# x_t in the order of the product's blocks, and wh in more banks, in a two-layer graph attention kernel

## What is computed

```python
def _gat_layer(x, W, adj):
    proj = x @ W                       # W: 256 x 512
    Wh, Ws = jnp.split(proj, 2, axis=-1)
    scores = Wh @ Ws.T                 # 4096 x 4096
    a = jax.nn.softmax(scores, axis=-1) * adj
    out = a @ Wh
    out = out + x
    return jax.nn.leaky_relu(out, 0.01)

y = _gat_layer(_gat_layer(x, W[0], adj), W[1], adj)
return _layernorm(x + y, axis=-1)      # eps 1e-5
```

## Time and profile before

| | us |
|---|---|
| median of 3 runs | 1680.99 (1677.59 to 1681.62) |
| the profiled execution's own time | 1675.62 |
| its span in the profile | 1673.7 |
| TensorE busy in the span | 1588.3 |
| VectorE | 1233.2 |
| GpSimd | 917.6 |
| ScalarE | 678.8 |
| mean granted TensorE clock | 0.99 of full speed |

### The profile page before, as it was taken

How to read it: one execution, slowest core, us unless ns; L and a number is a source line. 1 busy time by engine, 2 the same in 40 slices (tenths; PEclk the granted TensorE clock), 3 DMA queues, 4 the chain that set the end, 5 groups by cost and what they waited for, 6 DMA issues and landing times.

```text
span 1673.7 us, 23474 instructions
## 1 busy us (share of the span) xinstructions
PE 1588.3 (95%) x8104; PEld 1319.3 (79%) x8104; DVE 1233.2 (74%) x1558; ACT 678.8 (41%) x1175; POOL 917.6 (55%) x935
## 2 busy tenths in 40 slices
PE   7899999999999999999788999999999999999996
PEld 6778888888788888887677888888788888877885
DVE  4567777777777777777636788778878888787785
ACT  4333444444434444444333444344434444434442
POOL 2355555555555555555444555555555555555565
PEclk9999999999999999999999999999999999999998
DMA  5357767777767776768913777777677777777774
GB/s 182 86 147 185 193 185 184 186 198 182 184 186 192 184 186 187 195 186 220 261 32 105 193 192 184 192 201 194 177 191 202 196 186 189 197 190 185 199 192 126
DMA packets 167750, 302.59 MB, mean 181 GB/s; under 512 B 39760, under 2 KB 68432, under 8 KB 167504
## 3 DMA queue, kind: packets, MB, share of 16 engines
q1 hardware_dynamic: 105808, 132.75, 32.3%
q0 software_dynamic: 36864, 134.23, 27.6%
q10 hardware_dynamic: 24960, 34.11, 8.4%
HBM read 157.29 MB, written 9.44 MB: 100 GB/s over the span
## 4 chain that ended last, share of the span: by engine, by line
PE 55%; DVE 22%; ACTq 7%; POOL 6%; ACT 5%; issue 3%; DMA 1%; SPq 0%; POOLq 0%
PE banks L443 18%; PE banks L336 9%; PE banks L338 9%; PE banks L337 9%; PE banks L445 9%; DVE neg_max L641 8%; DVE ring L669 7%; ACTq L242 7%; POOL a_lo L766 6%; DVE ring L674 4%; ACT a_hi L559 3%; ACT ring L540 1%; DMA turned<-ring 1%; DVE weight L660 1%; DVE wh L605 1%
## 5 line engine op out<-in xcount | busy, mean ns | idle before, releaser
L766 POOL TENSOR_TENSOR a_lo<-turned,a_hi 128x512 fp32r<-128x512 f32 x512 | 718.4, 1419 | 667.3 <-ACT a_hi L559 666.8
L443 PE MATMUL banks<-wh,a_hi 128*128 128x512 f32 x2048 | 753.6, 406 | 50.7 <-POOL a_lo L766 43.2
L540 ACT ACTIVATE ring<-banks,neg_max 128x1024 f32<-128x1024 f32 x256 | 286.0, 1117 | 815.2 <-DVE neg_max L641 815.2
L445 PE MATMUL banks<-wh,a_lo 128*128 128x256 f32 x2048 | 577.5, 282 | 0.0
L443 PEld LDWEIGHTS banks<-wh,a_hi 128*128 128x128 f32 x2048 | 387.9, 189 | 182.6 <-POOL a_lo L766 83.0
L641 DVE TENSOR_REDUCE neg_max<-banks 128x1 f32<-128x1024 f32 x256 | 310.9, 1214 | 261.8 <-PE banks L338 261.8
L336 PE MATMUL banks<-x_t,q_t 128*128 128x512 f32 x1024 | 405.8, 396 | 4.0 <-DVE x_t L605 2.4
L338 PE MATMUL banks<-x_t,q_t 128*128 128x512 f32 x1024 | 401.8, 392 | 0.0
L337 PE MATMUL banks<-x_t,q_t 128*128 128x512 f32 x1024 | 400.9, 391 | 0.0
L445 PEld LDWEIGHTS banks<-wh,a_lo 128*128 128x128 f32 x2048 | 390.0, 190 | 5.8
L669 DVE SCALAR_TENSOR_TENSOR ring<-ring,weight,load 128x1024 f32<-128x1024 f32 x256 | 377.0, 1472 | 7.3 <-DMA load<-adj 4.6
(11 more groups left out here) (68 smaller groups left out, 729.6 us busy)
## 6 DMA issues: line engine op xcount, KB each, us to landing
load<-adj POOLq DMA_DIRECT2D x256, 512.0 KB, 5.0
turned<-ring SPq DMA_DIRECT2D x1528, 64.0 KB, 4.0
turned<-ring ACTq DMA_DIRECT2D x520, 64.0 KB, 4.0
ring<-x SPq DMA_DIRECT2D x8, 512.0 KB, 5.0
rows<-x SPq DMA_DIRECT2D x32, 128.0 KB, 4.3
x_scratch<-rows SPq DMA_DIRECT2D x32, 128.0 KB, 3.9
rows<-x_scratch SPq DMA_DIRECT2D x32, 128.0 KB, 4.3
first_rows<-x SPq DMA_DIRECT2D x32, 128.0 KB, 4.0
```

Source lines behind the costliest of these rows:

```text
L443: nc.tensor.matmul(psum[:, bank, :], a_hi[:, s, b], wh[:, k].rearrange("p a d -> p (a d)"), start=start, stop=stop, skip_group_check=True)
L445: last = nc.tensor.matmul(psum[:, bank, 0:D], a_lo[:, s, b], wh[:, k, 0], start=False, stop=stop, skip_group_check=True)
L540: nc.scalar.activation(ring[:, i % RING, :].rearrange("p (b e) -> p b e", b=2), psum[:, 2 * (i % 2):2 * (i % 2) + 2, :], ACT.Exp, bias=neg ...
L766: nc.gpsimd.tensor_tensor(a_lo[:, j % 2].rearrange("p b (r j) -> p b r j", r=QUADS), as_f32(turned[:, unit % 2, :, b:b + SUB, :]).rearrang ...
```

## The change

x_t holds the nodes in the order of the product's blocks: in each half of 2048 nodes, 16 blocks of 128, each of four runs of 32 that come from the half's four groups of 512. The splits of a transposed group write 16 runs of 32 nodes, 128 apart (group_nodes). A wh side takes 128 adjoining columns of x_t as they are, and picked, pick_columns and the semaphore columns_picked are gone. The scores of a bank read their moving operand as 8 runs of 64 columns (bank_nodes), q sides read theirs as 8 runs of 32 (pair_nodes). The columns of a chunk in the banks are then in another order; the exponentials write them back in the nodes' own order, in runs of 32, so that the ring, the adjacency matrix and all behind them are as before.

The wh of layer 0 are made in steps 0 to 5, as 3, 3, 3, 3, 2 and 2, those of layer 1 after the scores of n = 3, 4 and 5, as 3, 3 and 2; the eight before LATE_GROUP stay. The wh sides of layer 0 and the last eight of layer 1 may use banks 4 to 7, all other sides 4 and 5. A side takes the bank that was used longest ago and waits for the split of the side that had it. The split of a no longer waits for the last wh's matmuls.

```diff
--- before.py
+++ after.py
@@ -93,15 +94,31 @@
         SIDE_BANK, ACC_BANK = 4, 6
 
 
-
         W_SLOT = 4
         w_rows = [ring[:, W_SLOT + layer, :].rearrange("p (k e) -> p k e", k=KT) for layer in range(LAYERS)]
         w_t = [[turned[:, layer].rearrange("p r b j -> p (r b j)")[:, part * CHUNK:(part + 1) * CHUNK]
                 .rearrange("p (b c) -> p b c", b=2) for part in range(2)] for layer in range(LAYERS)]
         w_made = [[w_part[:, part] for part in range(2)],
                   [load[:, part].bitcast(F32R).rearrange("p (k e) -> p k e", k=KT) for part in range(2)]]
-        picked = [buf.rearrange("p s b j -> p (s b j)").rearrange("p (a k b j) -> p a k b j", a=2, k=KT, b=2)
-                  for buf in (a_hi, a_lo)]
+
+        def half_of_nodes(part, kt, half):
+            return x_t[:, part, kt, half * UNIT:(half + 1) * UNIT]
+
+        def group_nodes(part, g):
+            half, r = divmod(g % GROUPS, QUADS)
+            return (x_t[:, part, :, half * UNIT:(half + 1) * UNIT]
+                    .rearrange("p k (b r j) -> p k r b j", r=QUADS, j=QUAD)[:, :, r])
+
+        def bank_nodes(part, kt, c, b):
+            at = c % 2 * 2 * QUAD
+            return (half_of_nodes(part, kt, c // 2).rearrange("p (b e) -> p b e", e=P)
+                    [:, b * BLOCKS // 2:(b + 1) * BLOCKS // 2, at:at + 2 * QUAD])
+
+        def pair_nodes(part, kt, pair):
+            half, of = divmod(pair, PAIRS // 2)
+            r, b = of // 2, of % 2 * BLOCKS // 2
+            return (half_of_nodes(part, kt, half).rearrange("p (b r j) -> p r b j", r=QUADS, j=QUAD)
+                    [:, r, b:b + BLOCKS // 2])
 
         pool_step, ident_done = sem("pool_step"), sem("ident_done")
         w_loaded = [sem(f"w_loaded{layer}") for layer in range(LAYERS)]
@@ -110,7 +127,6 @@
         w_next_stored, w_next_loaded = sem("w_next_stored"), sem("w_next_loaded")
         x_loaded = [sem(f"x_loaded{s}") for s in range(10)]
         xt_done, xt_hi, xt_lo = sem("xt_done"), sem("xt_hi"), sem("xt_lo")
-        columns_picked = sem("columns_picked")
         side_done, side_hi, side_lo = sem("side_done"), sem("side_hi"), sem("side_lo")
         adj_loaded = sem_pair("adj_loaded")
         scores_done, max_done, exp_done = sem("scores_done"), sem("max_done"), sem("exp_done")
@@ -186,17 +202,18 @@
             return X_TURNS.get(step, [])
 
 
+        EARLY = WPAIRS // 2
+        WH_AFTER = [{0: 3, 1: 3, 2: 3, 3: 3, 4: 2, 5: 2}, {3: 3, 4: 3, 5: 2}]
+
         def sides_before(step):
-            return [("wh", WPAIRS + v) for v in range(WPAIRS // 2)] if step == LATE_GROUP else []
+            return [("wh", WPAIRS + v) for v in range(EARLY)] if step == LATE_GROUP else []
 
         def sides_after(step):
             made = []
             for layer in range(LAYERS):
-                n = step - layer * OFFSET
-                if layer == 0 and 0 <= n < WPAIRS // 2:
-                    made += [("wh", 2 * n), ("wh", 2 * n + 1)]
-                if layer == 1 and 3 <= n < 3 + WPAIRS // 4:
-                    made += [("wh", WPAIRS + WPAIRS // 2 + 2 * (n - 3) + v) for v in range(2)]
+                n, counts = step - layer * OFFSET, WH_AFTER[layer]
+                first = layer * (WPAIRS + EARLY) + sum(counts[v] for v in counts if v < n)
+                made += [("wh", first + v) for v in range(counts.get(n, 0))]
                 if n == -1 and layer:
                     made.append(("q", layer * PAIRS))
                 if n >= 0 and n % 8 == 6 and n // 8 + 1 < PAIRS:
@@ -210,6 +227,16 @@
 
         side_order = [("q", 0)] + [s for step in range(STEPS) for s in sides_before(step) + sides_after(step)]
         side_place = {s: n for n, s in enumerate(side_order)}
+
+
+        side_bank, side_last, last_in = {}, {}, {bank: None for bank in range(SIDE_BANK, SIDE_BANK + 4)}
+        for s in side_order:
+            kind, n = s
+            wide = kind == "wh" and (n < WPAIRS or n >= WPAIRS + EARLY)
+            side_bank[s] = min(range(SIDE_BANK, SIDE_BANK + (4 if wide else 2)),
+                               key=lambda bank: -1 if last_in[bank] is None else last_in[bank])
+            side_last[s] = last_in[side_bank[s]]
+            last_in[side_bank[s]] = side_place[s]
 
 
 
@@ -381,10 +408,9 @@
 
             def make_side(side):
                 kind, n = side
-                place = side_place[side]
-                bank = SIDE_BANK + place % 2
-                if place >= 2:
-                    pe.wait_ge(side_lo, place - 1)
+                bank = side_bank[side]
+                if side_last[side] is not None:
+                    pe.wait_ge(side_lo, side_last[side] + 1)
                 if kind == "q":
                     layer, pair = n // PAIRS, n % PAIRS
                     if pair == 0:
@@ -395,19 +421,25 @@
                         else:
                             pe.wait_ge(w_lo, 4)
                     for dt in range(KT):
-                        cols, of = slice(D + dt * P, D + (dt + 1) * P), slice(2 * P * pair, 2 * P * (pair + 1))
+                        cols = slice(D + dt * P, D + (dt + 1) * P)
                         last = three_products(
                             psum[:, bank, dt * 2 * P:(dt + 1) * 2 * P],
-                            [(w_part[:, 0, kt, cols], w_part[:, 1, kt, cols], x_t[:, 0, kt, of], x_t[:, 1, kt, of])
+                            [(w_part[:, 0, kt, cols], w_part[:, 1, kt, cols], pair_nodes(0, kt, pair), pair_nodes(1, kt, pair))
                              for kt in range(KT)])
                 else:
-                    pe.wait_ge(columns_picked, n + 1)
-                    of = picked[n % 2]
+                    layer, first = n // WPAIRS, 2 * (n % WPAIRS)
+                    half, b = first // BLOCKS, first % BLOCKS
+                    if b == 0:
+                        pe.wait_ge(xt_lo, layer * GROUPS + (half + 1) * GROUPS // 2)
+                    if layer and bank >= ACC_BANK:
+
+                        pe.wait_ge(acc_free, TILES - 1 + bank - ACC_BANK)
                     for t in range(2):
+                        of = slice((b + t) * P, (b + t + 1) * P)
                         last = three_products(
                             psum[:, bank, t * D:(t + 1) * D],
-                            [(of[:, 0, kt, t], of[:, 1, kt, t], w_part[:, 0, kt, 0:D], w_part[:, 1, kt, 0:D])
-                             for kt in range(KT)])
+                            [(half_of_nodes(0, kt, half)[:, of], half_of_nodes(1, kt, half)[:, of],
+                              w_part[:, 0, kt, 0:D], w_part[:, 1, kt, 0:D]) for kt in range(KT)])
                 last.then_inc(side_done, 1)
 
             def scores(i):
@@ -422,9 +454,8 @@
                     pe.wait_ge(exp_done, i - 1)
                 q = q_t[:, t // 2 % 2, :, :, t % 2 * P:(t % 2 + 1) * P]
                 for b in range(2):
-                    cols = slice(c * CHUNK + b * BANK, c * CHUNK + (b + 1) * BANK)
                     last = three_products(psum[:, 2 * (i % 2) + b, :],
-                                          [(q[:, 0, kt], q[:, 1, kt], x_t[:, 0, kt, cols], x_t[:, 1, kt, cols])
+                                          [(q[:, 0, kt], q[:, 1, kt], bank_nodes(0, kt, c, b), bank_nodes(1, kt, c, b))
                                            for kt in range(KT)])
                 last.then_inc(scores_done, 1)
 
@@ -503,13 +534,13 @@
 
                     act.wait_ge(scores_done, CHUNKS)
                     act.wait_ge(side_done, side_place["q", PAIRS - 1] + 1)
-                at = g % GROUPS * GROUP
-                nc.scalar.activation(x_t[:, 0, :, at:at + GROUP], psum[:, pair:pair + 2, :], ACT.Copy).then_inc(xt_hi, 1)
+                nc.scalar.activation(group_nodes(0, g), psum[:, pair:pair + 2, :].rearrange("p k (b j) -> p k b j", j=QUAD),
+                                     ACT.Copy).then_inc(xt_hi, 1)
 
             def split_side(side):
                 kind, n = side
                 place = side_place[side]
-                bank = psum[:, SIDE_BANK + place % 2, :]
+                bank = psum[:, side_bank[side], :]
                 act.wait_ge(side_done, place + 1)
                 if kind == "q":
                     nc.scalar.activation(q_t[:, n % 2, 0], bank.rearrange("p (k n) -> p k n", k=KT),
@@ -537,8 +568,9 @@
                             act.wait_ge(xt_done, g + 1)
                 elif i % RING >= W_SLOT:
                     act.wait_ge(w_lo, 4)
-                nc.scalar.activation(ring[:, i % RING, :].rearrange("p (b e) -> p b e", b=2),
-                                     psum[:, 2 * (i % 2):2 * (i % 2) + 2, :], ACT.Exp,
+                nc.scalar.activation(ring[:, i % RING, :].rearrange("p (r b j) -> p b r j", r=2, j=QUAD),
+                                     psum[:, 2 * (i % 2):2 * (i % 2) + 2, :].rearrange("p h (b r j) -> p (h b) r j", r=2, j=QUAD),
+                                     ACT.Exp,
```

(33 more changed lines are left out.)

## The result

The changed kernel takes 1670.49 us (median of 7 runs, 1667.55 to 1673.07) against 1680.99 for the kernel before: ratio 0.9939, interval 0.9924 to 0.9954. Beside each other on another occasion it was 1671.80 against 1677.80, ratio 0.9954 (0.9936 to 0.9972). By the ratios the change is worth 10.3 and 7.7 us, with intervals that reach from 5 to 13 (the medians lie 10.5 and 6.0 apart); the forecast was 7.6, 1673.5 in a range of 1668 to 1682. The profiled execution took 1670.49 us, with a span of 1668.1.

What follows compares the result with a forecast made beforehand. TensorE bounds the kernel, but at the layer starts VectorE's 6.8 us step holds it back and the first product waits for the last wh. Terms -6.5 - 1.1 = -7.6 us from 1680.99 gave 1673.4, given as 1673.5; range 1668 to 1682.

Steps and rivals of the forecast that it cites:

- the walk of layer 0: Layer 0 queues: first weigh later, at 58.6, but first product at 79.7 against 86.26; gain 6.5 us, also at scores 8.
- The clock's term: Lower clock level on the first product after the stall: 2.2 us charged in layer 0, 2.6 in layer 1.
- rival 1: Both layers: lower clock misses the product, gain 12.4 us (1668.6), chance 0.12 for that; both paid in full, 5.4 (1675.6).
- Zero for the order of x_t: Score and q operands, exponentials and x splits in runs: taken as 0; upper bound 11 us on the score matmuls.
- Zero for the picks in themselves: Removing GpSimd's 128 copies: worth nothing to 0.5 us in themselves, taken as 0.
- Rival 4: Layer 0: chunk 1's moves land after 77.7, holding up ScalarE's split; 4 us late leaves gain 5; 0.26 with another rival.
- VectorE's 6.8 us a step: Layer 0, steps 4 and 5: VectorE's period with two sides stays 6.8 us, putting step 6's weigh at 72.2.
- bound for a move: SP, chunk 1: a move takes at most 1.1 us on average, the last landing by 78.5; no wait taken.

Runs made afterwards that it cites:

- warm: Changed kernel plus 18 (layer 0) and 13 (layer 1) unread 512-column matmuls behind the scores of n = 7: 1667.53 us, ratio 0.9928 to before.
- order_kept_wait: Changed kernel with the old share, banks 4 and 5, and the old wait of the split of A for the last wh: 1682.10 us, ratio 1.0007 to before.
- schedule_only: Kernel before, with its picks and its order of x_t, given the new share of wh and the four banks: 1672.53 us, ratio 0.9963 to before.
- fours: Changed kernel with four wh in each of steps 0 to 3 (layer 1: n = 3 and 4), none after: 1674.08 us, ratio 0.9969 to before.
- late_again: Second run of the unchanged late_splits kernel: 1659.25 us, ratio 0.9889 to before.
- late_splits: Changed kernel with VectorE's split of each wh side from n = 3 on moved into the next step, behind weigh and turn: 1659.73 us, ratio 0.9885 to before.
- two_banks: Changed kernel with its new share of wh, but all sides on banks 4 and 5: 1679.81 us, ratio 0.9998 to before.

## Why the prediction was right

The trace of the changed kernel answers to the walk of layer 0 almost row by row; to compare, take 1.97 us off its times, by which scores 0 start later. First weigh 58.56 (forecast 58.6); weigh of step 6 at 72.22 (72.2); first product 79.75 (79.7), behind GpSimd's a_lo; stall 5.12 (5.1). The steps 0 to 3 were to be 7.05 us each and are 7.1. In layer 1, product 31.26 behind scores 3 (forecast 31.2), stall 3.60 (3.6). Gains at the products 6.5 and 3.7, forecast 6.5 and 3.7; at scores 8, 6.8 and 1.2, forecast 6.5 and 1.1. It is these rows that bear the mechanism out. That the total was met as well, 7.6 against 7.7 and 10.3 by the ratios, is partly luck, since the two occasions differ by a third.

- **The clock's term** was charged at what the old stall had cost, 2.2 and 2.6. It was 4.74 - 2.8 = 1.9 and 5.26 - 2.8 = 2.5, and warm, where the product starts at the same place and the lower level does not come, showed that it is the clock. Of rival 1 (the better outcome, 12 us), this profile has nothing. In the changed kernel's second profile the term was 1.4 in layer 0 and 2.5 in layer 1.
- **Zero for the order of x_t**: order_kept_wait shows it, within its interval. The Trainium skill's sentence on non-contiguous patterns (Advanced Engine Details and Errata, Memory Cachelines) is said of PSUM, and here it does not extend to a moving operand read from SBUF in runs of 64 words: 396 ns before and after. That is also what the same section asks of SBUF, more than one hit on a line.
- **Zero for the picks in themselves**: right in the kernel before, where two sides a step left time. With three a step they cost 1.8 us in layer 0 (schedule_only), so the zero hangs on the share.
- **Rival 4**, the moves, stayed out at VectorE's 6.8 us a step, and came in fours, where it is 3.6. The prediction's bound for a move was 1.1 us; it takes 0.64, and by the changed kernel's rows chunk 1 had landed at 75.4, well before ScalarE asked for it at 79.6.
- **Where the spans don't add up.** 6.8 + 1.2 = 8.0, but the spans differ by 5.6. The rest lies outside the change: the start, where scores 0 came 2.0 us later, and some tenths elsewhere. Windows over the start, and over the passage between the layers (from the last scores of layer 0 to those of n = 3), first of the kernel before, then of the changed one, then of the changed one's second profile:

```profile
9.00:14.00 5.00, 4.32 (x36) 4.08 (x36) 3.79 (x5) 3.90 (x6) 0.00 (x0) 1.00 0.96 292
...
801.70:876.52 74.82, 58.27 (x350) 49.90 (x348) 37.52 (x44) 27.60 (x42) 35.54 (x53) 0.95 0.54 147
```

```profile
9.00:14.00 5.00, 4.88 (x23) 4.88 (x24) 2.58 (x4) 1.84 (x4) 0.00 (x0) 1.00 0.76 249
...
796.70:871.43 74.73, 60.06 (x351) 51.53 (x349) 37.24 (x45) 27.47 (x42) 23.91 (x21) 0.93 0.53 145
```

```profile
795.85:868.34 72.49, 58.11 (x351) 49.77 (x349) 38.14 (x45) 27.49 (x42) 23.89 (x21) 0.98 0.54 150
```

From 9 to 14 us the record of the granted clock says 1.00 in both, but the changed kernel has fewer matmuls in it (23 against 36), and its first twelve of 256 columns start 0.21 us apart where those of the kernel before start 0.12 apart. That looks like the lower level, which this record does not show. It is not the change's doing: in the changed kernel's second profile scores 0 start at 27.94, as before. The passage is as long as before in the first profile and 2.3 us shorter in the second, at a clock of 0.98 instead of 0.93. Single profiles differ by such amounts; the ratios, which average over them, gave 7.7 and 10.3 us.

The prediction's weak place is not a term but what it left open: it took VectorE's 6.8 us a step as given and asked only what the change does under it. That wait for ScalarE inside a step, with the clock's lower level that its stalls brought on, was worth as much as the whole change or more: 12 us against 8 to 10.

## What to carry to other kernels

When an in-order engine has a step of its own work and then waits for another engine's half of a small job, move the second half behind the next step's own work: here, with four banks and three sides a step, that was worth 12 us, while the removal of 46 us of copies from an engine that nobody waited for was worth nothing. Buffers, share per step and place of the split depend on each other: the new share on two banks and the four banks with the old share each brought nothing beyond the freed wait, the late splits on two banks 5 us with the old share (the freed wait among them) and nothing at all with the new one, and everything together 19. Walk the in-order queues from one anchor with the rows' durations up to the point where the old and new order meet again, and compare there and not at the first instruction that moves, since what comes after a stall may run at the clock's lower level.

## What the runs showed of the hardware that had not been expected

A matmul whose moving operand is eight runs of 64 fp32 words (256 columns: eight runs of 32), and a ScalarE activation that writes runs of 32 words, take as long as with whole operands: 396 and 1117 ns both ways (q's matmuls 284, before 291, with different shares of the lower clock in it).

The same stall is not followed by the same clock in every execution. The 2.37 us before the scores of n = 3 in layer 1 stand in both profiles of the kernel with late splits. In the second (late_again) the clock was at its lower level behind it and the step took 1.6 us longer, in the first (late_splits) not; the windows, in this order, begin 0.5 us behind the start of the scores:

```profile
865.20:868.20 3.00, 3.00 (x9) 2.35 (x9) 0.00 (x0) 0.00 (x0) 0.00 (x0) 0.58 0.00 0
```

```profile
868.40:871.40 3.00, 3.00 (x18) 2.55 (x17) 0.43 (x1) 0.00 (x0) 0.00 (x0) 1.00 0.00 0
```

The longer stalls differ in it as well: 3.60 us before a product brought the lower level (the changed kernel), 3.51 did not (two_banks, layer 0). Over the passage between the layers the mean granted clock was 0.95 in the kernel before and 0.93 and 0.98 in the two profiles of the changed one, with the same work but for the copies [the windows above].

The executions of one kernel spread over 3.6 to 12.2 us, but those of late_splits over 0.8 (four executions) and 1.8 us (five, late_again). That its two stalls are gone is not shown to be the reason: warm has its clock up at the same places and spreads over 4.4 us.
